# Exchanging the 32x32 blocks of the turned probabilities: sixteen SBUF-to-SBUF transfers per half in place of a spill to DRAM and four reads

## The chip, the cores and the metric

The kernel runs on one core of one Trainium2 chip. The metric is the device time of one execution in microseconds. Before the change it was 897.46 us (median of 3 runs, 897.05 to 898.23). The profile comes from one further execution of 903.37 us.

## What is computed

A gated cross-attention layer is followed by a gated feed-forward layer, for 8 sequences of 128 tokens of width 512, all in float32:

```python
n = rmsnorm(layernorm(x)) * ln_weight                     # (8, 128, 512)
q, k, v = n @ w_q.T, ctx @ w_k.T, ctx @ w_v.T             # 32 heads of 128
score = softmax(where(mask, q @ k.T + position_bias, -inf))
attn = where(mask, score, 0) @ v                          # per sequence and head
x = x + tanh(g_xattn) * (layernorm(x) + attn @ w_out.T)
y = layernorm(x)
x = x + tanh(g_ffn) * (y @ base_W.T + lora of the top 2 of 28 experts)
```

The product of probabilities and values needs the probabilities with the keys on the partitions, while the softmax leaves them with the queries there. So each 128x128 tile of probabilities is turned (transposed) once. How the turned tile is put together is what the change touches.

## The kernel before, in words

Two heads make a phase, and there are 16 phases. The q projections of phases 1 to 15 are made first (to about 197 us of the span) and spilled to DRAM. Then a loop runs over p = 1 to 15 (`iteration` on each engine). In it the attention of phase a = p-1 is finished, while the k and v projections of phase p are made. p = 15 is written out apart, and the feed-forward layer follows it.

A phase has four units u: head u%2 of the phase, and half t = u//2 of the batch, four sequences each. In iteration p the queues hold this, in order:

- TensorE: the scores of the four units (line 1165); the k chunks 0 to 3 and the first v chunk (line 1134); `pv(a, 0)` and `pv(a, 1)` (line 1193), which read `probs_t` of half 0; three more v chunks; `pv(a, 2)` and `pv(a, 3)`, which read half 1; and eight output projections. `pv` waits on `block_in[t]` before it starts.
- VectorE: bias and row maximum per unit (lines 912, 915); after ScalarE's exponentials the division by the row sum (lines 921 to 926); and per half one transpose of 32x32 blocks (`turn_probs`, line 932) from `attn` into `block_sb`. That instruction turns each 32x32 block in place; the blocks themselves still have to change places across the partitions, which `exchange` does.
- SyncE (SP): all DMAs of the loop, in this order: the q of phase p (`load_q`, line 308, 1 MB), `exchange` of half 0, `exchange` of half 1, the bias, and the weights of k, v and the output (`refill`, line 232). Each refill waits until GpSimd has read the weights that it replaces.

In `exchange(a, t)` SP waits for the transpose, writes the whole of `block_sb[t]` (128 partitions x 4 KB) to a DRAM buffer, waits until that has landed, and reads it back in four DMAs, one for each group of 32 destination partitions (32 partitions x 4 pieces of 1 KB). In `probs_t` it is then block (m, k) of `block_sb` that stands at block (k, m).

The order of the work is written out by hand on every engine; there is no planner.

Of the kernel before, what the change touches and what calls it, by code (L numbers as in the profile page):

```python
# [16 lines left out]
F32 = mybir.dt.float32  # L17
# [7 lines left out]
P = 128  # L25
# [8 lines left out]
HP = 2  # L34
# [3 lines left out]
BU = B // 2  # L38
# [7 lines left out]
Q32 = 32  # L46
NB = S // Q32
# [12 lines left out]
def build(nc, x, ctx_t, weights, bias, mask, g_x, g_f, ln_w, out):  # L60
    ctx = ExitStack()
    with ctx:
# [3 lines left out]
        def sem(name):  # L66
            return ctx.enter_context(nc.semaphore(name))
# [45 lines left out]
        probs = attn[:, 0:UNITS * BU * S].rearrange("p (n b s) -> p n b s", n=UNITS, b=BU)  # L113
        probs_t = attn[:, UNITS * BU * S:].rearrange("p (t a n q) -> p t a n q", t=2, a=NB, n=HP * BU)
        blocks = [block_sb[:, t, :].rearrange("p (a n q) -> p a n q", a=NB, n=HP * BU) for t in range(2)]
        block_spill = [nc.dram_tensor(f"block_spill{t}", (P, NB, HP * BU * Q32), F32, kind="Internal").ap() for t in range(2)]
        xt_raw = attn[:, :].rearrange("p (c t) -> p c t", c=C)
        q_buf = attn[:, 0:HP * T].rearrange("p (j t) -> p j t", j=HP)
        v_sum, w_copy, t_sum = attn[:, 5 * HALF:6 * HALF], attn[:, 6 * HALF:7 * HALF], attn[:, 7 * HALF:8 * HALF]
# [39 lines left out]
        def pv_bank(a, u):  # L159

            if isinstance(a, int) and a >= LAST - 1:
                return pv_ps if a == LAST else (turn_ps, pv_ps)[u % 2]
            return (turn_ps, pv_ps, score_ps[0], score_ps[1])[u]
# [50 lines left out]
        scores_done, biased, max_done = sem("scores_done"), sem("biased"), sem("max_done")  # L214
        exp_done, scaled, probs_done = sem("exp_done"), sem("scaled"), sem("probs_done")
        turned, turn_copied, blocks_done = sem("turned"), sem("turn_copied"), sem("blocks_done")
        block_out, block_in = ([sem(f"block_{n}{t}") for t in range(2)] for n in ("out", "in"))
        pv_done, at_hi_done, at_split = sem("pv_done"), sem("at_hi_done"), sem("at_split")
        out_done, first_share = sem("out_done"), sem("first_share")

# [9 lines left out]
        def _(sp):  # L230
# [80 lines left out]
            def exchange(a, t):  # L311

                sp.wait_ge(blocks_done, a * 2 + (t + 1))
                sp.dma_start(block_spill[t], blocks[t].rearrange("p a n q -> p a (n q)")).then_inc(block_out[t], 16)
                sp.wait_ge(block_out[t], a * 16 + 16)
                for k in range(NB):
                    rows = slice(k * Q32, (k + 1) * Q32)
                    sp.dma_start(probs_t[rows, t, :, :, :].rearrange("p a n q -> p a (n q)"),  # L318
                                 block_spill[t][:, k, :].rearrange("(a k) n -> k a n", k=Q32)).then_inc(block_in[t], 16)

            load_bias(1)
            for k in (WK, WV):
# [4 lines left out]
            with sp.Fori(1, LAST) as p:  # L327
                load_q(p)
                for t in range(2):
                    exchange(p - 1, t)  # L330
                load_bias(p + 1)
                refill(WK, p + 2)
                refill(WV, p + 2)
                refill(WO, p + 1)
            load_q(LAST)
            for t in range(2):
                exchange(LAST - 1, t)
# [788 lines left out]
        def _(pe):  # L1126
# [52 lines left out]
            def pv(a, u):  # L1179

                j, t = u % HP, u // HP
                if isinstance(a, int) and a == LAST:
                    pe.wait_ge(turn_copied, u + 1)

                    pe.wait_ge(at_split, a * UNITS + u)
                else:
                    pe.wait_ge(block_in[t], a * (16 * NB) + 16 * NB)
                    if isinstance(a, int) and a == LAST - 1 and u >= 2:

                        pe.wait_ge(at_split, a * UNITS + (u - 1))  # L1190
                for i in range(BU):
                    b = t * BU + i
                    mm = pe.matmul(pv_bank(a, u)[:, i * S:(i + 1) * S], v_sb[:, b, j * DH:(j + 1) * DH], probs_t[:, t, :, j * BU + i, :],  # L1193
                                   start=True, stop=True)
                mm.then_inc(pv_done, 1)
# [163 lines left out]
            def iteration(p):  # L1359
# [30 lines left out]

                pe.wait_ge(proj_copied, so_far(p))
                pv(a, 0)
                pv(a, 1)
                chunk(UNITS + 1)
                chunk(UNITS + 2)
                chunk(UNITS + 3)
                pv(a, 2)
                pv(a, 3)
                pe.wait_ge(w_lo_done[WO], p)
# [189 lines left out]
```

## Time and profile before

| | |
|---|---|
| median of 3 runs | 897.46 us |
| the profiled execution: its time, its span | 903.37 us, 901.6 us |
| TensorE busy | 871.0 us, 97% of the span |
| VectorE, ScalarE, GpSimd busy | 486.7, 358.9, 301.2 us |
| DMA packets | 50673, 109.69 MB, 37.0% of the 16 engines' span |
| block_spill<-block_sb | 30 DMAs of 512 KB |
| attn<-block_spill | 120 DMAs of 128 KB (`probs_t` and `probs` both lie in the tensor `attn`) |

The profile names tiles without buffer numbers and by the tensor they lie in. So pv of units 0 to 3 stands as turn_ps, pv_ps, score_ps, score_ps <- attn, v_sb at line 1193, and the scores as turn_ps, pv_ps, score_ps <- kt, qt at line 1165. "Busy" shares are averages over the span; what ends each wait is read from the chain and from the waits.

### The profile page before, as it was taken

How to read it: one execution, taken by the hardware profiler on the slowest of the kernel's cores; microseconds unless marked ns; L12 is line 12 of the kernel's file. 1: busy time of each engine (PE TensorE's matmuls, PEld its weight loads, DVE VectorE, ACT ScalarE, POOL GpSimd, SP SyncE). 2: the span in 40 equal slices, each digit the busy share in tenths (PEclk: the TensorE clock that was granted, in tenths of full speed). 3: DMA queues.
4: the chain of work that ended last, by engine and by line, in shares of the span. 5: the costliest groups of instructions: out<-in, count | busy, mean ns of one | idle time of the engine just before them, and what ended most of it. 6: DMA issues, size and time to landing. Idle time of an engine off the chain costs nothing.

```text
span 901.6 us, 15022 instructions
## 1 busy us (share of the span) xinstructions
PE 871.0 (97%) x5128; PEld 769.5 (85%) x5128; DVE 486.7 (54%) x847; ACT 358.9 (40%) x966; POOL 301.2 (33%) x216
## 2 busy tenths in 40 slices
PE   8999999998999999999999999999999999999998
PEld 7878888887888988898989889898889898898786
DVE  6886565573627272636354362726263535577863
ACT  5654444553434342425253343434242525354320
POOL 1476665663232323314132323232231413332200
PEclk9999999999999999999999999999999999999999
DMA  9134545555243333424251524333342425151101
GB/s 312 39 105 158 179 151 175 174 176 198 67 150 99 116 116 99 154 85 146 69 183 37 187 65 151 110 105 122 108 148 76 154 61 190 35 201 34 38 24 70
DMA packets 50673, 109.69 MB, mean 122 GB/s; under 512 B 6752, under 2 KB 24160, under 8 KB 48736
## 3 DMA queue, kind: packets, MB, share of 16 engines
q1 hardware_dynamic: 50656, 109.47, 37.0%
q8 instruction: 10, 0.16, 0.1%
q14 instruction: 7, 0.06, 0.0%
HBM read 75.89 MB, written 33.55 MB: 121 GB/s over the span
## 4 chain that ended last, share of the span: by engine, by line
PE 64%; DMA 14%; DVE 12%; issue 4%; SPq 2%; ACT 1%; POOL 1%; DVEq 0%; POOLq 0%
PE proj_ps L1134 34%; PE proj_ps L1307 15%; DMA block_spill<-block_sb 9%; DMA attn<-block_spill 5%; DVE attn L912 3%; PE score_ps L1193 3%; PE proj_ps L1485 2%; PE turn_ps L1193 2%; PE pv_ps L1193 2%; DVE block_sb L932 2%; SPq L318 2%; DVE attn L926 2%; PE turn_ps L1165 1%; PE proj_ps L1503 1%; DMA acc<-in_x 1%
## 5 line engine op out<-in xcount | busy, mean ns | idle before, releaser
L372 POOL TENSOR_TENSOR w_lo<-w_raw,w_hi 128x1024 fp32r<-128x1024 f32 x49 | 117.1, 2391 | 312.9 <-ACT w_hi L466 312.8
L1134 PE MATMUL proj_ps<-w_hi,ct_hi 128*128 128x256 f32 x512 | 146.4, 286 | 0.0
L1134 PE MATMUL proj_ps<-w_hi,ct_lo 128*128 128x256 f32 x512 | 145.0, 283 | 0.0
L1134 PE MATMUL proj_ps<-w_lo,ct_hi 128*128 128x256 f32 x512 | 145.0, 283 | 0.0
L383 POOL TENSOR_TENSOR comb<-mask_add,bias_sb 128x1024 f32<-128x1024 f32 x32 | 76.7, 2417 | 131.4 <-DVE attn L926 127.6
L486 ACT ACTIVATE attn<-attn,neg_max 128x128 f32<-128x128 f32 x256 | 99.2, 389 | 52.6 <-DVE neg_max L915 52.6
L948 DVE TENSOR_TENSOR acc<-proj_ps,acc 128x512 f32<-128x512 f32 x112 | 77.5, 692 | 66.7 <-PE proj_ps L1134 65.8
L466 ACT ACTIVATE w_hi<-w_raw 128x1024 fp32r<-128x1024 f32 x49 | 51.8, 1059 | 121.9 <-PE proj_ps L1134 118.9
L1134 PEld LDWEIGHTS proj_ps<-w_hi,ct_hi 128*128 128x128 f32 x512 | 98.4, 192 | 0.7
L1134 PEld LDWEIGHTS proj_ps<-w_hi,ct_lo 128*128 128x128 f32 x512 | 98.3, 192 | 0.7
L1134 PEld LDWEIGHTS proj_ps<-w_lo,ct_hi 128*128 128x128 f32 x512 | 98.2, 192 | 0.0
L1134 PE MATMUL proj_ps<-w_hi,tf_hi 128*128 128x512 f32 x240 | 95.3, 397 | 0.0
L1134 PE MATMUL proj_ps<-ct_hi,w_hi 128*128 128x512 f32 x240 | 94.7, 395 | 0.0
L1134 PE MATMUL proj_ps<-w_lo,tf_hi 128*128 128x512 f32 x240 | 93.7, 390 | 0.0
L1134 PE MATMUL proj_ps<-ct_hi,w_lo 128*128 128x512 f32 x240 | 93.5, 390 | 0.0
L1134 PE MATMUL proj_ps<-ct_lo,w_hi 128*128 128x512 f32 x240 | 93.5, 389 | 0.0
L1134 PE MATMUL proj_ps<-w_hi,tf_lo 128*128 128x512 f32 x240 | 93.4, 389 | 0.0
L944 DVE TENSOR_TENSOR tf_lo<-score_ps,tf_hi 128x512 fp32r<-128x512 f32 x28 | 19.4, 692 | 126.8 <-ACT tf_hi L492 126.8
L944 DVE TENSOR_TENSOR tf_lo<-turn_ps,tf_hi 128x512 fp32r<-128x512 f32 x16 | 11.1, 691 | 95.5 <-ACT tf_hi L492 95.5
L416 POOL TENSOR_TENSOR w_lo<-w_raw,w_hi 128x256 fp32r<-128x256 f32 x60 | 47.3, 791 | 26.7 <-ACT w_hi L557 26.5
L1134 PEld LDWEIGHTS proj_ps<-w_lo,tf_hi 128*128 128x128 f32 x240 | 45.0, 188 | 9.7
L1134 PEld LDWEIGHTS proj_ps<-ct_lo,w_hi 128*128 128x128 f32 x240 | 45.0, 188 | 9.4
(204 smaller groups left out, 1781.2 us busy)
## 6 DMA issues: line engine op xcount, KB each, us to landing
w_raw<-in_weights SPq DMA_DIRECT2D x67, 512.0 KB, 3.7
q_spill<-attn SPq DMA_DIRECT2D x60, 256.0 KB, 3.0
qt<-q_spill SPq DMA_DIRECT2D x15, 1024.0 KB, 7.9
block_spill<-block_sb SPq DMA_DIRECT2D x30, 512.0 KB, 4.0
attn<-block_spill SPq DMA_DIRECT2D x120, 128.0 KB, 2.9
acc<-in_x SPq DMA_DIRECT2D x4, 512.0 KB, 9.8
bias_sb<-in_bias SPq DMA_DIRECT2D x16, 128.0 KB, 2.9
out<-attn SPq DMA_DIRECT2D x8, 256.0 KB, 2.0
```

Source lines behind the costliest of these rows:

```text
L318: sp.dma_start(probs_t[rows, t, :, :, :].rearrange("p a n q -> p a (n q)"), block_spill[t][:, k, :].rearrange("(a k) n -> k a n", k=Q32)). ...
L372: pool.tensor_tensor(lo, w_raw[:, k, :], hi.bitcast(F32), ALU.subtract).then_inc(w_lo_done[k], 1)
L383: pool.tensor_tensor(comb[:, j, :, :], mask_add[:, :, :], bias_sb[:, j:j + 1, :].to_broadcast([P, B, S]), ALU.add).then_inc(comb_done, 1)
L416: pool.tensor_tensor(columns(w_lo, WO, n), columns(w_raw, WO, n), columns(w_hi, WO, n).bitcast(F32), ALU.subtract).then_inc(qs_lo, 1)
L466: act.activation(w_hi[:, k, :] if hi is None else hi, w_raw[:, k, :], ACT.Copy).then_inc(w_hi_done[k], 1)
L486: e = act.activation(probs[:, u, i, :], probs[:, u, i, :], ACT.Exp, bias=neg_max[:, u, i:i + 1], accum_out=row_sum[:, u, i:i + 1])
L912: dve.tensor_tensor(probs[:, u, :, :], score_bank(a, u)[:, :].rearrange("p (b s) -> p b s", b=BU), comb[:, j, t * BU:(t + 1) * BU, :], ALU ...
L944: dve.tensor_tensor(lo[to], pv_bank(a, u)[:, :], hi[to].bitcast(F32), ALU.subtract).then_inc(at_split, 1)
L948: dve.tensor_tensor(acc[:, b, :], proj_ps[b % BANKS][:, :], acc[:, b, :], ALU.add).then_inc(acc_done, 1)
L1134: mm = pe.matmul(o, lhs(l, n), rhs(r, n), start=(start and n == 0 and m == 0), stop=(stop and n == terms - 1 and m == 2))
L1193: mm = pe.matmul(pv_bank(a, u)[:, i * S:(i + 1) * S], v_sb[:, b, j * DH:(j + 1) * DH], probs_t[:, t, :, j * BU + i, :], start=True, stop=True)
L1307: mm = pe.matmul(o[:, :], w[l][:, c, :], x[r][:, c, :], start=(start and c == 0 and m == 0), stop=(c == 1 and m == 2), skip_group_check=no ...
```

## The change

The DRAM buffer and the semaphore of its write go. SP issues sixteen DMAs per half instead of one and four, each from 32 partitions of `block_sb` to 32 partitions of `probs_t`, 1 KB a partition. The value that TensorE waits for grows from 64 to 256 per phase. Nothing else is changed: order of the queue, buffers and the other engines' instructions stay.

```diff
-        block_spill = [nc.dram_tensor(f"block_spill{t}", (P, NB, HP * BU * Q32), F32, kind="Internal").ap() for t in range(2)]
...
-        block_out, block_in = ([sem(f"block_{n}{t}") for t in range(2)] for n in ("out", "in"))
+        block_in = [sem(f"block_in{t}") for t in range(2)]
...
             def exchange(a, t):
                 sp.wait_ge(blocks_done, a * 2 + (t + 1))
-                sp.dma_start(block_spill[t], blocks[t].rearrange("p a n q -> p a (n q)")).then_inc(block_out[t], 16)
-                sp.wait_ge(block_out[t], a * 16 + 16)
                 for k in range(NB):
-                    rows = slice(k * Q32, (k + 1) * Q32)
-                    sp.dma_start(probs_t[rows, t, :, :, :].rearrange("p a n q -> p a (n q)"),
-                                 block_spill[t][:, k, :].rearrange("(a k) n -> k a n", k=Q32)).then_inc(block_in[t], 16)
+                    for m in range(NB):
+                        sp.dma_start(probs_t[k * Q32:(k + 1) * Q32, t, m, :, :].rearrange("p n q -> p (n q)"),
+                                     blocks[t][m * Q32:(m + 1) * Q32, k, :, :].rearrange("p n q -> p (n q)")).then_inc(block_in[t], 16)
...
-                    pe.wait_ge(block_in[t], a * (16 * NB) + 16 * NB)
+                    pe.wait_ge(block_in[t], a * (16 * NB * NB) + 16 * NB * NB)
```

## Rows read from the trace of the kernel before

**Rows 1.** The page: busy time; the chain that ended last, by engine and by line.
```profile
PE 871.0 (97%) x5128; PEld 769.5 (85%) x5128; DVE 486.7 (54%) x847; ACT 358.9 (40%) x966; POOL 301.2 (33%) x216
...
PE 64%; DMA 14%; DVE 12%; issue 4%; SPq 2%; ACT 1%; POOL 1%; DVEq 0%; POOLq 0%
PE proj_ps L1134 34%; PE proj_ps L1307 15%; DMA block_spill<-block_sb 9%; DMA attn<-block_spill 5%; DVE attn L912 3%; PE score_ps L1193 3%; PE proj_ps L1485 2%; PE turn_ps L1193 2%; PE pv_ps L1193 2%; DVE block_sb L932 2%; SPq L318 2%; DVE attn L926 2%; PE turn_ps L1165 1%; PE proj_ps L1503 1%; DMA acc<-in_x 1%
```

**Rows 2.** Waits of TensorE: us in total, times, longest us.
```profile
PE turn_ps L1193 <- DMA attn<-block_spill: 18.4, 14, 4.4
```

**Rows 3.** Timeline of TensorE around both pv pairs of one phase: start, duration.
```profile
465.95 0.28 PE L1134 MATMUL proj_ps<-w_lo,ct_hi 128*128 128x256 f32 x1
467.07 1.16 PE L1193 MATMUL turn_ps<-attn,v_sb 128*128 128x128 f32 x8 [0.84 <-DMA attn<-block_spill]
468.88 0.36 PE L1134 MATMUL proj_ps<-w_hi,ct_hi 128*128 128x256 f32 x1
...
477.60 1.95 PE L1193 MATMUL score_ps<-attn,v_sb 128*128 128x128 f32 x16
479.31 0.47 PE L1134 MATMUL proj_ps<-w_hi,tf_hi 128*128 128x512 f32 x1
```

**Rows 4.** The same timeline: the first and last of the 14 waits, and phase 15.
```profile
214.56 1.70 PE L1193 MATMUL turn_ps<-attn,v_sb 128*128 128x128 f32 x8 [4.38 <-DMA attn<-block_spill]
...
759.73 1.16 PE L1193 MATMUL turn_ps<-attn,v_sb 128*128 128x128 f32 x8 [1.02 <-DMA attn<-block_spill]
...
802.09 1.06 PE L1193 MATMUL turn_ps<-attn,v_sb 128*128 128x128 f32 x8
```

**Rows 5.** The chain of waits, where it passes through one exchange: start, duration.
```profile
457.30 5.34 DMA block_spill<-block_sb
...
463.98 3.05 DMA attn<-block_spill
```

**Rows 6.** Timeline of SP's queue; x4 is four issues, first start to last end.
```profile
204.22 0.33 SPq L314 DMA_DIRECT2D block_spill<-block_sb  x1
...
462.66 1.75 SPq L318 DMA_DIRECT2D attn<-block_spill  x4
464.53 0.35 SPq L314 DMA_DIRECT2D block_spill<-block_sb  x1
...
470.70 23.90 SPq L232 DMA_DIRECT2D w_raw<-in_weights  x3
...
792.17 0.33 SPq L314 DMA_DIRECT2D block_spill<-block_sb  x1
...
800.47 0.34 SPq L314 DMA_DIRECT2D block_spill<-block_sb  x1
...
804.87 1.85 SPq L341 DMA_DIRECT2D w_raw<-in_x  x4
```

**Rows 7.** The page: issues, size, median us to landing; and line 318, all issues.
```profile
attn<-block_spill SPq DMA_DIRECT2D x120, 128.0 KB, 2.9
...
out<-attn SPq DMA_DIRECT2D x8, 256.0 KB, 2.0
...
DMA to landing us min/median/max: 2.6/2.9/3.7
```

**Rows 8.** DMA view of 55 to 57 us, in 40 slices; the issue is at 55.31.
```profile
GB/s 0 0 0 0 0 0 0 0 0 0 0 0 0 0 0 0 0 0 0 0 0 0 41 246 369 287 492 328 410 451 246 492 369 410 287 410 287 123 0 0
q_spill<-attn SPq DMA_DIRECT2D x1, 256.0 KB, 2.4
```

**Rows 9.** SP's queue at the start, when every load of the kernel is queued.
```profile
1.18 0.43 SPq L239 DMA_DIRECT2D qt<-in_ctx_t  x1
4.59 0.59 SPq L239 DMA_DIRECT2D kt<-in_ctx_t  x1
9.41 0.44 SPq L256 DMA_DIRECT2D gates<-in_g_x  x1
```

**Rows 10.** Window: PE, PEld, DVE, ACT, POOL busy, granted clock, DMA share, GB/s.
```profile
214.50:218.00 3.50, 3.44 (x18) 3.44 (x19) 0.69 (x1) 0.60 (x1) 1.02 (x1) 0.57 0.34 115
```

## The prediction

> **What bounds the kernel now.** I read the page first. TensorE is busy for 871.0 of 901.6 us [rows 1], so at most some 30 us are to be had without fewer matmuls. Yet the chain runs for 14% of the span through the two DMAs of the exchange, so what little idle time TensorE has is set by them. The waits say how much: 14 waits of TensorE for attn<-block_spill, 18.4 us in all, the longest 4.4 [rows 2]. The timeline shows the place. In each phase the last k/v matmul ahead of pv(a, 0) starts at 465.95, the next could start 0.12 later, at 466.07, and pv starts at 467.07 [rows 3]. That is 1.00 us late, which the view, counting from the modelled end, calls 0.84. A start after a wait also runs slower: from pv's start to the next projection it is 1.81 us for 16 matmuls, against 1.71 for the 16 of the second pair, which doesn't wait [rows 3]. So a wait that vanishes gives back its figure and 0.26 us. The first phase waits 4.38, the other thirteen (18.4 - 4.38)/13 = 1.08 on average [rows 2, 4]. The second pair (half 1) never waits [rows 3], nor does the fifteenth phase [rows 4].
>
> **The path that ends this wait.** Half 0's blocks are ready at 457.30. The write to DRAM lands 5.34 us later; the four reads are issued from 462.66, the last at 463.98, and that one lands after 3.05 us, at 467.03 [rows 5, 6]. From blocks to data, 9.73 us. Call that X. This phase's wait is 0.24 below the mean, so the mean X is 9.97; in the first phase it is 214.56 - 0.04 - 204.22 = 10.30 [rows 4, 6]. TensorE needs the data at 466.07, less 0.04 from landing to start [rows 3, 5]. So X = 8.73 is the mark: below it the wait is gone, and more speed buys nothing.
>
> **What the change puts there.** The write, the landing that SP waits for, and the reads go. Left are 16 issues and the landing of the last one.
>
> *Issues.* The x4 group takes 1.75 us with issues of 0.43 and 0.04 between, the first one 0.33: a step of 0.37, then steps of 0.47 [rows 6]. From the first issue to the sixteenth: 0.37 + 14 x 0.47 = 6.95 us. Bounds: if each costs what a lone issue costs (0.33 [rows 6]) the step is 0.37 and the sum 5.55. When the kernel starts and all loads are queued, 15 steps lead from 1.18 to 9.41, 0.55 each (the groups between hold 15 issues), and single ones reach 0.59 + 0.04 = 0.63 [rows 9]. In the loop one load, q's 1 MB, stands just ahead of the exchange in the queue and is in flight beside the first of the sixteen. I take 0.47: same queue, same stage, same 32 destination partitions.
>
> *Landing.* No row shows a transfer from SBUF to SBUF. The reads of 128 KB from DRAM take 2.9, the 256 KB stores of the result 2.0 [rows 7]. One 256 KB store on an idle queue can be split: issued at 55.31, first bytes at about 56.1, last at about 56.9, landed 2.4 after the issue [rows 8]. So 0.8 to the first byte, 0.8 of bytes, 0.8 of receipt. A piece of the change has an eighth of the bytes (0.1), which gives 1.7; from the 2.0 of the result's stores the same cut gives 1.3. I take 1.6. The ends I keep are 1.3 and 2.9.
>
> Together X = 6.95 + 1.6 = 8.55, under 8.73. The wait goes in the thirteen phases: 13 x (1.08 + 0.26) = 17.4 us. In the first phase it becomes shorter by 10.30 - 8.55 = 1.75. After that long wait the granted clock was 0.57 over 3.5 us, so mostly the lower of its two levels, 1.2 GHz [rows 10]: pv took 1.70 there against 1.16 [rows 4]. The 2.6 us that remain may or may not save that stretch (0 to 1.6 us), and I count nothing. Sum 19.1 us, to 884.2 in the profiled execution.
>
> *The Trainium skill* speaks less kindly of small transfers. "DMA: Bandwidth & Descriptors", section "Anatomy of one DMA", gives about 2.0 us plus the bytes at 436 GB/s for each DMA of the GpSimd path; the trace's 2.4 for 256 KB is close to its 2.6. By that a piece would take 2.08 and X would be 9.03, an estimate from that page; the case with a rest of the wait below is where it would lead.
>
> **What else moves.** *Half 1.* SP now has 16 issues of half 0 ahead of it: the first of half 1 can't go before 457.30 + 0.37 + 15 x 0.47 = 464.7, which is where its write goes now (464.53 [rows 6]); the last goes at 471.8 and lands at 473.4. pv(a, 2) is due at 477.60 less the 1.1 us that the phase gained, 476.5 [rows 3]. Cover 3.1 us; it is gone if a step costs over 0.57. *Queued behind.* Bias and weights follow. The first refill goes at 470.70, and the three together stretch over 23.9 us because the later ones wait for GpSimd, not for SP [rows 6]. So only the first comes about 2.2 us late, and its data are wanted in the next phase, a good 20 us on. Cost nothing; without that cover, 2.2 us a phase. *End.* In phase 15 half 0 starts at 792.17 and lands at 800.7, ahead of the 802.09 at which pv starts there [rows 4, 6]; cover 1.4 us. Half 1 starts at 800.47, so the reloads of x go at about 808.0 instead of 804.87 [rows 6]; I cost it at nothing, at worst 3 us if the residual waits. *DMA load.* 512 KB less pass twice through DRAM per half. The count of issues goes from 150 to 480. The 16 engines carry it: the issues space the bytes at 32 KB per 0.47 us, 70 GB/s, against 250 to 490 in the strip [rows 8]. *TensorE* waits in the same places as before; only the value differs.
>
> **From the profile to the runs.** The profiled execution is 5.9 us above the median shown. Matmul pace hardly differs between the two, so part of the 5.9 probably sits in the waits that this change removes: were it spread over the chain outside TensorE (36% of the span [rows 1], 325 us, of which 5.9 is 1.8%), the 18 us path from scores to pv would be 0.33 shorter in each of 14 phases, 4.6 us in all. I take off half, 2.3: gain 16.8, time 880.6.
>
> **Rivals.**
> 1. *A rest of the wait stays.* The landing takes the whole 2.0 of the result's stores [rows 7]: X = 8.95, 0.22 over the mark. Gain per phase 9.97 - 8.95 = 1.02 in thirteen, 1.35 in the first: 14.6, less the 2.3: 885.2. For it: the queue also holds q's megabyte. Against: both stores with few bytes taken off come out below it.
> 2. *Nothing is won.* Either steps of 0.55 as at the start [rows 9] (X = 15 x 0.55 + 1.6 = 9.85) or the landing of a DRAM read, 2.9 (X = 9.85). Gain 14 x 0.12 = 2: 895.5. Against: in the loop the steps are 0.47 while a 512 KB write has just been in flight, and no read of DRAM is left.
> 3. *Slower: each small transfer has a price above 0.57 us*, be it SP's issue or the engines' hand-over from one to the next. It strikes in half 0 of each phase. At the start single steps cost 0.63 [rows 9], and that is the nearest price above the point: X = 15 x 0.63 + 1.6 = 11.05, later by 1.08 in thirteen phases and 0.75 in the first, +14.8 us. Half 1 would land at 457.30 + 31 x 0.63 + 1.6 = 478.4, just in time. 912. For it: the four reads land 0.6 us apart on average if the first, which finds the engines idle, takes the shortest time of its kind, 2.6: (467.03 - 465.26)/3 [rows 5, 7]. Against: those carry 128 KB each, four times a piece. *The Trainium skill* ("DMA: Bandwidth & Descriptors", section "Bandwidth") has transfers under 64 KB dominated by their descriptors, with 0.68 us busy for 4 KB and 0.95 for 64 KB; were the pieces worked one after another at that, the estimate from it is a price of 0.7 to 0.9 and a case 3 of several times the size. The trace's steps of 0.47 are issues, and no row there shows such small transfers following each other.
> 4. *The transfers use fewer engines than 16*, so that the change isn't what it says. The reads now also go to 32 partitions and pull 128 KB in under 3 us [rows 7]; I give it little and the price of case 3.
>
> **How the numbers follow.** Forecast 45%, rest of the wait 20%, nothing won 12%, slower 23% (cases 3 and 4). A measurement tells from no change what exceeds 0.2%, 1.8 us. Forecast and case 1 are faster, half of case 2 too: 0.71; same 0.06; slower 0.23. The likeliest alone spans 876 (all 19.1 us, and the clock kept in the first phase) to 884. The range: 20% left out, most of it case 3 above: 876 to 900.
>
> **What would show it.** Right: the waits of TensorE for the exchange fall from 14 to one, of about 2.6 us, in the first phase; each phase is 1.3 us shorter; the chain of the loop stays on TensorE; sixteen issues take about 7.4 us; the last lands after 1.6. Rest: 14 waits of 0.1 to 0.5 us. Wrong: steps above 0.57 on SP, or landings that drift away from their issues (a last one that takes 3 us or more), or new waits at score_ps line 1193 for half 1.

## The result

The changed kernel takes 941.39 us (median of 4 runs, 939.85 to 943.23), against 897.48 before: ratio 1.049 (1.047 to 1.051). It is slower by 44 us. The forecast was 880.6, in a range of 876 to 900, and faster with a chance of 0.71. It was wrong in sign and outside the range. What came is the third rival by its mechanism, at three times its price.

The page of the changed kernel answers to [rows 1] with this:

```profile
span 939.8 us, 15338 instructions
PE 888.7 (95%) x5128; PEld 786.4 (84%) x5128; DVE 486.6 (52%) x847; ACT 358.5 (38%) x966; POOL 301.0 (32%) x216
...
PE 61%; SPq 16%; DVE 12%; issue 5%; DMA 4%; ACT 1%; POOL 1%; DVEq 0%; POOLq 0%
PE proj_ps L1131 31%; SPq L315 15%; PE proj_ps L1304 14%; DVE attn L909 3%; DMA attn<-block_sb 3%; PE turn_ps L1190 3%; PE pv_ps L1190 3%; PE score_ps L1190 3%; PE proj_ps L1482 2%; DVE block_sb L929 2%; DVE attn L923 2%; PE turn_ps L1162 1%; PE proj_ps L1500 1%; DMA acc<-in_x 1%; DVE row_scale L920 1%
...
attn<-block_sb SPq DMA_DIRECT2D x480, 32.0 KB, 1.8
```

The chain's share in DMA fell from 14% to 4%, and SP's own queue rose from 2% to 16%: line 315 is the issue of the sixteen transfers. The same number of matmuls keeps TensorE busy for 17.7 us more. That is the second half of the loss, and the waits are the first:

```profile
PE turn_ps L1190 <- DMA attn<-block_sb: 38.7, 16, 5.9
```

They were 18.4 us [rows 2], so 20.3 more. 20.3 and 17.7 make the 38.0 of the 38.2 by which the span grew. (The profiled execution of before was 5.9 us above its median, that of after is not; this is the rest of the 44.)

One phase of the chain of waits, against [rows 5] (start, duration; the sixteen issues of half 0 begin at 473.12, the sixteenth is the one at 482.56, and ten of them are left out):

```profile
473.12 0.52 SPq L315
473.65 0.06 issue
473.70 0.58 SPq L315
474.28 0.04 issue
474.32 0.59 SPq L315
474.92 0.04 issue
474.96 0.59 SPq L315
...
481.93 0.59 SPq L315
482.52 0.04 issue
482.56 1.83 DMA attn<-block_sb
484.40 0.04 issue
484.44 1.16 PE turn_ps L1190 x8
```

An issue takes 0.59 us, not 0.43, and the step is 0.635. Fifteen steps are 482.56 - 473.12 = 9.44 us, and the landing takes 1.83: X, from blocks to data, is 11.27, against 9.97 before and a mark of 8.73. The timeline of SP shows the same step for half 1, 32 issues in one go:

```profile
469.48 0.33 SPq L307 DMA_DIRECT2D qt<-q_spill  x1
473.12 20.17 SPq L315 DMA_DIRECT2D attn<-block_sb  x32
493.57 0.35 SPq L298 DMA_DIRECT2D bias_sb<-in_bias  x1
494.19 17.77 SPq L231 DMA_DIRECT2D w_raw<-in_weights  x3
```

The last of the 32 goes at 492.7 and lands at 494.5. TensorE starts on it at 494.96, so half 1 is hidden by 0.4 us. The strip of the DMA engines from 473 to 485 (40 slices, busy share in tenths) shows that they aren't what SP waits for: once q's load has gone no slice is busier than 0.4, and a third of them are at 0. The window below it has the mean, 0.20 (columns as in [rows 10]).

```profile
DMA  9995524031221303040404030302112130304040
...
475.10:482.60 7.50, 6.96 (x43) 6.06 (x41) 2.58 (x5) 3.55 (x10) 5.16 (x3) 1.00 0.20 51
```

What a wait does to TensorE is read from two phases. Columns as in [rows 3]:

```profile
484.44 1.16 PE L1190 MATMUL turn_ps<-attn,v_sb 128*128 128x128 f32 x8 [2.38 <-DMA attn<-block_sb]
...
527.54 1.50 PE L1190 MATMUL turn_ps<-attn,v_sb 128*128 128x128 f32 x8 [2.38 <-DMA attn<-block_sb]
```

and the windows behind them (columns as in [rows 10]; the granted clock is the third number from the end):

```profile
484.20:486.60 2.40, 2.16 (x19) 2.16 (x20) 0.34 (x1) 0.67 (x2) 0.31 (x1) 1.00 0.22 55
527.20:529.00 1.80, 1.46 (x9) 1.46 (x10) 0.00 (x0) 0.00 (x0) 0.42 (x1) 0.78 0.21 52
529.00:531.00 2.00, 2.00 (x12) 2.00 (x11) 0.69 (x1) 0.81 (x2) 0.00 (x0) 0.50 0.20 51
531.00:533.00 2.00, 2.00 (x16) 2.00 (x16) 0.69 (x1) 0.87 (x2) 0.00 (x0) 0.84 0.20 49
533.00:535.00 2.00, 2.00 (x19) 2.00 (x19) 0.00 (x0) 0.60 (x1) 0.00 (x0) 1.00 0.20 49
```

Both phases wait 2.38 us. Behind the one the clock stays at 1.00, and the phase takes 43.1 us from scores to scores. Behind the other it is 0.50, the level of 1.2 GHz, for some three microseconds, and the phase takes 44.7. Of the thirteen phases after the first, eleven went the second way and two the first. 11 x 1.6 us is 17.6, against the 17.7 of TensorE's longer busy time.

### The profile page after: what moved, and what is told of

Its sections match the earlier page's. It is cut to its first block, busy times and chain, and to the rows that moved or that the text cites. A ratio compares the mean times of both kernels' runs of the same rounds, so it can differ in the third digit from the quotient of the medians.

```text
span 939.8 us, 15338 instructions
## 1 busy us (share of the span) xinstructions
PE 888.7 (95%) x5128; PEld 786.4 (84%) x5128; DVE 486.6 (52%) x847; ACT 358.5 (38%) x966; POOL 301.0 (32%) x216
## 4 chain that ended last, share of the span: by engine, by line
PE 61%; SPq 16%; DVE 12%; issue 5%; DMA 4%; ACT 1%; POOL 1%; DVEq 0%; POOLq 0%
PE proj_ps L1131 31%; SPq L315 15%; PE proj_ps L1304 14%; DVE attn L909 3%; DMA attn<-block_sb 3%; PE turn_ps L1190 3%; PE pv_ps L1190 3%; PE score_ps L1190 3%; PE proj_ps L1482 2%; DVE block_sb L929 2%; DVE attn L923 2%; PE turn_ps L1162 1%; PE proj_ps L1500 1%; DMA acc<-in_x 1%; DVE row_scale L920 1%
## 5 line engine op out<-in xcount | busy, mean ns | idle before, releaser
L1131 PE MATMUL proj_ps<-w_hi,ct_hi 128*128 128x256 f32 x512 | 148.5, 290 | 0.9 <-ACT kt L468 0.7
L1190 PE MATMUL turn_ps<-attn,v_sb 128*128 128x128 f32 x128 | 26.7, 374 | 38.7 <-DMA attn<-block_sb 38.7
L1190 PEld LDWEIGHTS turn_ps<-attn,v_sb 128*128 128x128 f32 x128 | 22.5, 264 | 41.9 <-DMA attn<-block_sb 40.3
```

The costliest lines, as they stand in the source:

```text
L1131: mm = pe.matmul(o, lhs(l, n), rhs(r, n), start=(start and n == 0 and m == 0), stop=(stop and n == terms - 1 and m == 2))
```

## The experiments

Three sets of runs, with the kernel before measured beside each (896.8, 901.3 and 901.1 us). The first four ask what makes a step long, which half pays, and what the clock takes.

### Sixteen small reads, from DRAM

```diff
                 sp.wait_ge(block_out[t], a * 16 + 16)
                 for k in range(NB):
-                    sp.dma_start(probs_t[rows, t, :, :, :]..., block_spill[t][:, k, :]...)
+                    for m in range(NB):
+                        sp.dma_start(probs_t[k * Q32:(k + 1) * Q32, t, m, :, :]..., block_spill[t][m * Q32:(m + 1) * Q32, k, :])
```

> The kernel before with one edit: the write to DRAM stays, but each of the four reads becomes four reads of 32 KB, so sixteen of the shape of the changed kernel's transfers (32 partitions x 1 KB) with DRAM as source. It separates what makes SP's step 0.63 us in the changed kernel and 0.47 before. Theory A: SBUF on both sides is what costs (0.59 a DMA). Then these sixteen take 0.43 each, a step of 0.47, and the last lands about 5.3 + 7.0 + 2.6 = 14.9 us after the blocks are ready. Theory B: the small shape is what costs (two rows per engine). Then the step is 0.63 here too, and the last lands after about 17.5. Either way TensorE waits some 5 or 8 us per phase, at half clock after it: by A about 990 us, by B about 1030.

Measured: 986.19 us, ratio 1.099 (1.095 to 1.103). The chain through one exchange (left out are twelve of the sixteen issues):

```profile
442.48 5.07 DMA block_spill<-block_sb
447.55 0.02 issue
447.57 0.33 SPq L318
447.90 0.04 issue
447.94 0.42 SPq L318
448.36 0.04 issue
448.41 0.42 SPq L318
...
454.43 1.71 DMA attn<-block_spill
```

The step is 0.46, with the shape, the size and the count of the changed kernel. So neither the small transfer nor its two rows per engine make the 0.635. The last lands at 456.14, 13.7 us after the blocks: a read of 32 KB lands in 1.7, where I had counted 2.6. Theory A holds (986 for about 990), with this one term taken too long.

### Four wide transfers on chip

```diff
                 for k in range(NB):
-                    for m in range(NB):
-                        sp.dma_start(probs_t[k * Q32:(k + 1) * Q32, t, m, :, :]..., blocks[t][m * Q32:(m + 1) * Q32, k, :, :]...)
+                    sp.dma_start(probs_t[:, t, k, :, :]..., blocks[t][:, k, :, :]...)
```

> The changed kernel with four transfers per half instead of sixteen, each 128 partitions x 1 KB from SBUF to SBUF. It leaves out the exchange across partitions (each block lands on the partitions it came from). Theory A (SBUF on both sides makes an issue cost 0.59): a step of 0.63 between the four. Theory B (the small shape does): a step of 0.47. Either way blocks to data is about 0.6 + 2 x 0.6 + 2.1 = 3.9 us, well under the mark of 8.73, so TensorE no longer waits for the exchange: the profiled time falls from 903.4 by 19 to about 884, the median to about 880. If the waits are not what costs, the time stays at 897.

This kernel leaves out the exchange across the partitions. Measured: 880.16 us, ratio 0.981 (0.978 to 0.983). In SP's timeline the first issue and the three behind it:

```profile
444.63 0.48 SPq L314 DMA_DIRECT2D attn<-block_sb  x1
...
445.17 1.88 SPq L314 DMA_DIRECT2D attn<-block_sb  x3
```

1.88 us hold three issues of 0.60 and two gaps: a step of 0.64 at 128 partitions too. With the first run this settles A: in the loop an issue costs SP 0.42 to 0.43 where DRAM is the source, and 0.59 to 0.60 with SBUF on both sides, there at 32 rows as at 128. What in the queue takes the 0.16 no run shows. The time also confirms the other part of the prediction, the worth of the wait: 896.8 - 880.2 = 16.6 us, and one wait of the fourteen is left, of 0.8 us.

### Half 1 alone by direct transfers

```diff
+                if t == 1:
+                    for k in range(NB):
+                        for m in range(NB):
+                            sp.dma_start(probs_t[k * Q32:(k + 1) * Q32, t, m, :, :]..., blocks[t][m * Q32:(m + 1) * Q32, k, :, :]...)
+                    return
                 sp.dma_start(block_spill[t], ...)
```

> One part of the change alone: half 0 goes through DRAM as before, half 1 goes by the sixteen direct transfers. Theory: only half 0 stands on the path. SP is free for half 1 at 464.5, sixteen steps and a landing end at 464.5 + 9.5 + 1.8 = 475.8 in the phase of the rows, ahead of TensorE's need at 477.6. So 897 us, within 2 of before, and 14 waits for attn<-block_spill of 18 us in all. Rival: the extra 4.5 us of SP's queue also cost, by a late half 1 or by late loads behind it: 1 us or more per phase, 912 or above, with new waits at score_ps line 1193 or at w_hi.

Measured: 897.75 us over 10 runs, ratio 1.0005 (0.999 to 1.002).

```profile
PE turn_ps L1200 <- DMA attn<-block_spill: 13.8, 12, 3.9
...
PE turn_ps L1200 <- DMA attn<-block_sb: 0.2, 1, 0.2
...
259.50:261.50 2.00, 2.00 (x11) 2.00 (x11) 1.19 (x2) 1.08 (x2) 0.00 (x0) 0.50 0.22 54
```

240 of the change's 480 transfers cost nothing when they follow an exchange through DRAM, and in the changed kernel every wait of the thirteen phases is one for half 0. So the loss sits in half 0. The expectation of 14 waits and 18 us was too high for this execution: twelve waits, 13.8 us. One of them, 1.99 us in the second phase, had the low clock behind it (the window above, columns as in [rows 10]), and that phase took 44.3 us.

### Matmuls in place of the wait

```diff
                 pe.wait_ge(proj_copied, so_far(p))
+                pe.wait_ge(biased, a * UNITS + 1)
+                for _ in range(FILL):      # FILL = 9
+                    pe.matmul(turn_ps[:, :], ct_hi[:, 0, 0:P], ct_hi[:, 0, 0:HALF], start=True, stop=True)
                 pv(a, 0)
```

> The changed kernel, and in each of the 14 phases of the loop nine matmuls of 128x512 (0.23 us each, 2.0 us) that nobody reads stand ahead of pv(a, 0), where TensorE waits 2.4 us. They take no time that is not waiting. Theory C: of the 38 us that the change cost, some 18 are matmuls at half clock after each wait of 2.4 us. Then with the filler the waits shrink to about 0.3 us, the clock stays at 1.00 behind them, and the time falls from 941 by 15 to 20, to about 924. Rival: the clock falls for another reason than the wait (or its loss is hidden behind the next exchange): the time stays at 939 to 942.

Measured: 924.87 us, 16.5 less than the changed kernel; ratio to before 1.030 (1.028 to 1.033). TensorE's timeline in one phase:

```profile
431.24 2.23 PE L1392 MATMUL turn_ps<-ct_hi 128*128 128x512 f32 x9
433.78 1.16 PE L1191 MATMUL turn_ps<-attn,v_sb 128*128 128x128 f32 x8 [0.31 <-DMA attn<-block_sb]
```

All thirteen phases now take 43.1 us, the length of the two above whose clock stayed at 1.00. The data come no earlier; work that nobody reads has made the kernel faster by 16.5 us, because TensorE didn't stand still. So the 44.7 of the others hold 1.6 us of clock each, and it is the standing still that took it. Why two of the thirteen waits of 2.38 us were spared, no run shows.

The other six ask what gets the gain that was forecast.

### Twelve direct transfers

The blocks (k, k) don't change partitions. VectorE turns these four straight into `probs_t`.

```diff
-                    for m in range(NB):
+                    for m in [m for m in range(NB) if m != k]:
                         sp.dma_start(...)
...
+                for k in range(NB):
+                    rows = slice(k * Q32, (k + 1) * Q32)
+                    to = dve.transpose(probs_t[rows, t, k, :, :], probs[rows, HP * t:HP * t + HP, :, rows]...)
+                to.then_inc(diag_done, 1)
```

> The changed kernel with twelve direct transfers per half in place of sixteen; the four blocks that stay on their partitions are turned straight into place by four small VectorE transposes behind the large one. Theory: what the change costs is the number of issues times 0.635 us. Eleven steps: 0.58 + 10 x 0.635 + 1.83 = 8.76 us from blocks to data instead of 11.3, 0.03 over the mark. So waits of TensorE of 0 to 0.2 us instead of 2.4, the clock at 1.00, and 880 to 884: faster than before by 13 to 17, though it is the same exchange. Rival: something else than the count of issues (the shared queue behind q's load, half 1's lateness) holds the time: over 900.

Measured: 888.00 us, ratio 0.984 (0.982 to 0.987). Phases of 40.6 us instead of 44.7, clock 1.00, and one wait left in the loop:

```profile
PE turn_ps L1197 <- DMA attn<-block_sb: 3.2, 1, 3.2
```

Four issues fewer per half are worth over 50 us against the changed kernel, since they bring X from one side of the mark to the other. The expectation was 4 to 8 us too low. It had left out the first phase, where the wait of 3.2 and the slow clock behind it make 46.8 us against the 41.6 of the four wide transfers, and the last, whose tail is 1.5 us longer. The first phase of the kernel before took 46.7, so there the shorter wait (3.2 against 4.4) won nothing: from 213 to 219 us the granted clock is 0.51 here, against 0.72 before.

### Turning on VectorE alone, both halves and half 0

```diff
-                dve.transpose(blocks[t]..., probs[:, HP * t:HP * t + HP, :, :]...).then_inc(blocks_done, 1)
+                for k in range(NB):
+                    for m in range(NB):
+                        to = dve.transpose(probs_t[k * Q32:(k + 1) * Q32, t, m, :, :],
+                                           probs[m * Q32:(m + 1) * Q32, HP * t:HP * t + HP, :, k * Q32:(k + 1) * Q32]...)
+                to.then_inc(blocks_done, 1)
```

SP's exchange goes. In the second kernel this holds for t = 0 only, and half 1 goes through DRAM.

> No DMA in the exchange at all: sixteen VectorE transposes per half, each from 32 partitions straight to 32 other partitions of probs_t, in place of the one over 128 partitions. If a transpose of a quarter of the rows costs 0.35 us (the large one, four times the elements a row, takes 1.25), a half costs 5.6 us on VectorE instead of 1.25. Data are there 5.6 us after the last division, 4.4 us ahead of TensorE's need. VectorE gets 8.7 us a phase more, of 41, and half 1 comes 4.4 + 4.4 us later on it, with some 5 us of cover left. Theory: the wait goes as in the other kernels, 878 to 882, less what the last phase loses where VectorE is on the path (up to 6): 878 to 888. Rival: VectorE becomes late for half 1 or for the next scores: waits at score_ps line 1190, above 890.

> Half 0 turned by sixteen small VectorE transposes straight into place, half 1 through DRAM as before. Theory: half 0 alone stands on the path, so this gets all of the gain (878 to 884), with half of VectorE's extra time. Rival: half 1, later by 4.4 us on VectorE and then 9 us through DRAM (ready at about 467, data at about 475, need at 476.5), becomes the wait: 14 waits at score_ps line 1193.

Measured: 887.90 us (0.984, 0.982 to 0.986) and 887.73 us (0.984, 0.982 to 0.987). The first is at the upper end of its range. The second is 3.7 us above its range (878 to 884), though its mechanism holds: half 0 alone gets the gain of the loop. The small transposes are dearer than I took them for:

```profile
444.96 7.18 DVE L927 STREAM_TRANSPOSE attn<-attn 32x256 f32<-32x256 f32 x16
```

0.45 us each, 7.2 a half, where 0.35 and 5.6 were expected. Even so TensorE doesn't wait for the exchange in the thirteen phases after the first; they are 40.47 us in both. The first phase is 42.5 and 43.3 us, against 41.6 of the four wide transfers. Most is lost in the last: from its scores to the end it is 124.6 and 123.2 us, against 118.5 there. VectorE is on the path there: between 761 and 800 us the chain of the first kernel runs for 34% through the small transposes, while that of the four wide transfers, between 759 and 798, has 2% on VectorE. In the second kernel TensorE also waits there for half 1's reads from DRAM:

```profile
PE turn_ps L1201 <- DMA attn<-block_spill: 1.8, 1, 1.8
```

### The order instead of the route

```diff
-                pv(a, 0)
-                pv(a, 1)
                 chunk(UNITS + 1)
+                pv(a, 0)
+                pv(a, 1)
                 chunk(UNITS + 2)
```

> The kernel before (exchange through DRAM), with one edit in TensorE's order: in the loop, pv(a, 0) and pv(a, 1) stand behind one more v chunk (2.9 us of matmuls). The exchange keeps its 10.0 us from blocks to data; the mark moves from 8.73 to 11.6. Theory: only that wait is to be had, so it goes in thirteen phases, and the first keeps about 1.5 of its 4.4 us: the waits for attn<-block_spill fall from 18.4 to under 2 us and the time from 897 to 878 to 880, as with the four wide transfers that were never waited for (880.2). Rival: the later pv makes ScalarE's and VectorE's chain late (at_hi, at_split, the output projections), and half of the gain or more comes back as waits of the output projection: 886 or above.

Measured, on the kernel before: 880.95 us, ratio 0.978 (0.976 to 0.980). The exchange still goes through DRAM, with the same five DMAs, and TensorE waits 0.8 us for it in all:

```profile
PE turn_ps L1193 <- DMA attn<-block_spill: 0.8, 1, 0.8
```

This is the lowest time of a kernel that computes everything, and it is faster than both given ones.

On the changed kernel the same edit:

> The changed kernel (sixteen direct transfers per half), with pv(a, 0) and pv(a, 1) behind one more v chunk. The mark for half 0 moves to 11.6 us, the data come at 11.3: that wait goes. Theory: all 32 issues of a phase stand in one queue, so half 1 is the next to be late. Its last transfer is issued 19.6 us after the blocks of half 0 are ready and lands at 21.4; TensorE, no longer held up by half 0, comes for it at 19.2. So 13 new waits of 2.2 us at score_ps line 1190, with or without the half clock behind them (0 to 1.6 us a phase): 912 to 934 us. Rival: half 1 is hidden as before the edit, and with half 0 covered the kernel comes to 880.

Measured: 939.24 us, ratio to before 1.042 (1.038 to 1.045), 2 us less than without.

```profile
PE score_ps L1190 <- DMA attn<-block_sb: 27.4, 13, 2.1
PE turn_ps L1190 <- DMA attn<-block_sb: 5.0, 3, 3.0
```

The wait has moved to half 1 as the theory has it, 2.1 us for 2.2 expected. So the change had a second limit 0.4 us behind the first: 32 issues in one queue. The clock fell behind all thirteen waits (phases of 44.4), which the upper end of the range had allowed for. That the time is 5 us above that end comes from what I had added nothing for: the first phase, 46.6 us where the kernel below has 41.4, and the tail, 121.1 from the last scores where the four wide transfers have 118.5.

On the kernel with twelve:

> Twelve direct transfers per half, and pv(a, 0) and pv(a, 1) behind one more v chunk. Half 0 needs 8.8 of 11.6 us; half 1's last transfer is issued 0.5 + 22 x 0.635 = 14.5 us after half 0's blocks and lands at 16.4, due at 19.2. Theory: nothing of the exchange is waited for, also in the first phase, where the twelve alone lost 5 us; left of the twelve's cost is the last phase (1 us). 880 to 882, the same as the DRAM route with the same edit (880.95): once it is hidden, the route is worth nothing. Rival: the direct route is better where both are hidden, by its smaller load of DRAM: 878 or less.

Measured: 881.99 us, ratio 0.979 (0.976 to 0.981), as the theory had it. Phases of 40.47, a wait of 0.5 us in the first, and 1.5 us of tail. Hidden, the two routes are worth the same to 1 us; the intervals of the two ratios don't tell them apart.

## Why the prediction was wrong, by its steps

**What bounds the kernel: right.** Half 0's exchange was the one wait of the loop; half 1's costs nothing (the half 1 run), and removing the wait is worth 17 to 20 us (to 880.2 from the 896.8 of its set, and to 880.95 from 901.3; I had said 16.8 after the discount). The mark was right as well: with X at about 8.8 the phases take 40.6, with none to wait for 40.47. The thirteen phases of before took 543.6 us, those of the four wide transfers 526.2, and the difference of 17.4 is the term of the sum. That the forecast's 880.6 is the time of the kernels without a wait is in part luck. They also shorten the first phase by 5 us, where I counted 1.75, and in the kernel with twelve transfers, whose X is the nearest to my 8.55, the first phase gains nothing and the time is 888.0.

**The step that failed is the issue.** "0.37 + 14 x 0.47 = 6.95". It measured 9.44: 2.5 us of error on a quantity with 0.18 us of room to the mark. I took the step from the reads that the change removes, for "same queue, same stage, same 32 destination partitions". They differ in the one thing that counts, the side they read from. No row had SBUF on both sides, as I wrote for the landing, and I did not apply that to the issue. The rows from the start of the kernel (0.55, 0.63) have DRAM as source too, so they gave nearly the right size for another reason, which stays open; the changed kernel has its step with engines that are busy for a fifth of the time.

**The landing:** 1.83 for 1.6, inside the bounds. The estimate from the Trainium skill ("DMA: Bandwidth & Descriptors", section "Anatomy of one DMA"), 2.08, missed it by as much on the other side; this trace's 1.83 decides.

**Rival 3** set its price at 0.63 us, and said 14.8 us for it. By X alone that holds: 13 x (11.27 - 9.97) = 16.9. What was missing is the clock. The prediction treats it for the first phase only, as something that a shorter wait may give back, and never asks what a longer one costs in the others: 17.6 us, as much again. *The estimate from the Trainium skill* for this case ("DMA: Bandwidth & Descriptors", section "Bandwidth", whose figures are for loads from HBM issued by GpSimd), pieces worked one after another by the engines at 0.68 to 0.95 us, isn't what happened: the engines were busy for 0.20 of the time, and the step is the issue's 0.635.

**Rival 4**, fewer engines than 16, isn't it either. In 40 slices of 475.10 to 482.60 the share of the sixteen reaches 0.6, so at least ten work at once:

```profile
DMA  0133005005102400600330150051024005004201
```

**What else moves:** half 1 in time by 0.4 us (I had "just in time" for this case), the loads behind it harmless. Phase 15 was taken as free; TensorE waits 1.5 us there, and from the last scores to the end it is 120.8 us against 118.6.

**From profile to runs:** the before of this case ran at 897 or 901 us in different sets, each on another chip, while the kernels without the wait stay at 880 to 882. That fits a wait that depends on how fast DRAM answers, but neither this nor the chip's own part was tried.

**The chances** were the gravest fault. With 0.18 us of room, and a price bounded between 0.37 and 0.63, the bounds of X were 7 to 11, with the mark and the break-even (0.57) in the middle. That isn't 71% faster.

## What to carry to other kernels

Count issues before bytes: what replaces a few DMAs by many small ones moves the cost to the issuing queue, and the price of one must come from a transfer with the same memories on both sides. Where a transfer must be ready at a mark, compare the spread of the estimate with the room, and price both sides, the far one with TensorE's clock: a wait of 2.4 us made most phases 4 us longer than none. If a wait is to go, look first for work of the waiting engine that can stand ahead of it; one line moved gave the whole gain here, with the slow route left as it was.

## What the runs showed of the hardware

- A DMA issued by SP in the loop, one behind the other: 0.42 to 0.43 us with DRAM as source, 0.59 to 0.60 from SBUF to SBUF, at 32 KB as at 128 KB. At the start of the kernel loads from DRAM took 0.43 to 0.59 [rows 9]; why is open.
- Reads of 32 KB from DRAM land in 1.7 us and SBUF-to-SBUF transfers of 32 KB in 1.8: at this size the way on chip is no quicker per transfer. At 128 KB it was 2.9 and 2.1, in different shapes (32 partitions of 4 KB, 128 of 1 KB).
- After waits for the exchange of 2.0 to 2.4 us the granted clock fell to 0.50 in most phases, but not in all (11 of 13 in the changed kernel, 13 of 13 with pv later, once in the half 1 run). After the thirteen waits of 0.75 to 1.54 us before the change it never did.
- A VectorE transpose may read one group of 32 partitions and write another, at 0.45 us for 32 x 256; the one over 128 x 1024 takes 1.25.
